# New written orders for TensorE's instruction stream in an attention and expert layer, and the expert weights computed four groups earlier

## What is computed

```python
xn = layernorm(x)                          # x: 2 x 2048 x 256
q, k, v = split(xn @ Wqkv)                 # 16 heads of 16, rotary embedding on q and k
attn = softmax(causal(q @ k.T * scale)) @ v
p = softmax(xn @ gate_w.T + gate_b)        # 10 gates: 8 experts, 2 null ones
w, chosen = top_k(p, 2)                    # null choices weigh nothing, the rest is normalised
ffn = sum over the two choices: w * (xn @ expert_w[chosen] + expert_b[chosen])
out = x + attn @ Wout + bout + ffn
```

## Time and profile before

| | us |
|---|---|
| median of three runs | 1015.39 |
| the profiled execution | 1015.35 |
| span of its instructions | 1013.6 |
| TensorE busy | 909.3 |
| VectorE busy | 846.4 |
| ScalarE busy | 727.5 |
| GpSimd busy | 462.7 |
| `attend`: group 0, first score to that of group 1 | 91.5 |
| group 3 | 106.4 |
| group 6 | 96.2 |
| group 7 | 89.3 |

### The profile page before, as it was taken

The page is one execution under the profiler, slowest core; times in us unless marked ns, Lnnn a source line. Parts: engine busy times, 40 slices in busy tenths (PEclk is TensorE's granted clock), DMA queues, the critical chain, the costliest instruction groups (busy, mean ns, idle before and its releaser), DMA issues. The chain is left out here.

```text
span 1013.6 us, 22104 instructions
## 1 busy us (share of the span) xinstructions
PE 909.3 (90%) x7874; PEld 389.5 (38%) x7874; DVE 846.4 (83%) x1096; ACT 727.5 (72%) x1542; POOL 462.7 (46%) x588
## 2 busy tenths in 40 slices
PE   3888445999999999999999999999999799999988
PEld 1544311333433244344443544353434233323257
DVE  6999789899889988886888788877888599994856
ACT  3556200888778888888888788878887688799922
POOL 4677659555200343344834564255222344355610
PEclk9999765899999999999999999999999899999989
DMA  9776810300200323244413542265323321022113
GB/s 324 267 256 238 285 51 6 111 2 26 68 14 2 106 85 126 78 135 145 126 54 114 151 143 76 70 167 134 82 75 118 97 60 54 23 64 64 43 42 125
DMA packets 82084, 106.65 MB, mean 105 GB/s; under 512 B 10000, under 2 KB 59064, under 8 KB 80952
## 3 DMA queue, kind: packets, MB, share of 16 engines
q1 hardware_dynamic: 74488, 85.83, 26.3%
q0 software_dynamic: 6528, 17.83, 6.7%
q10 hardware_dynamic: 960, 1.57, 0.5%
HBM read 67.37 MB, written 37.50 MB: 103 GB/s over the span
## 5 line engine op out<-in xcount | busy, mean ns | idle before, releaser
L1272 DVE TENSOR_REDUCE blk<-psP 128x2 f32<-128x1024 f32 (+2 forms) x576 | 640.9, 1161 | 102.1 <-PE psP L1415 52.0
L1218 ACT ACTIVATE probs<-psS 128x512 f32<-128x512 f32 (+3 forms) x1280 | 589.0, 540 | 163.8 <-PE psS L1455 157.9
L1455 PE MATMUL psS<-Qs,Ks 50*128 50x512 f16 (+3 forms) x1280 | 331.6, 354 | 13.4 <-ACT probs L1218 8.9
L1415 PE MATMUL psP<-Ks,Qs 48*128 48x512 f16 (+3 forms) x1280 | 295.8, 363 | 27.9 <-DVE blk L1272 17.3
L1511 PE MATMUL psO<-probs,Vs 128*32 128x512 f32 (+3 forms) x2560 | 302.7, 548 | 11.1 <-POOL probs L1119 10.1
L1119 POOL TENSOR_SCALAR_AFFINE_SELECT probs<-probs 128x512 f32<-128x512 f32 x128 | 88.1, 689 | 333.7 <-ACT probs L1218 251.3
L1455 PEld LDWEIGHTS psS<-Qs,Ks 50*128 50x128 f16 x1280 | 96.0, 93 | 252.8 <-ACT probs L1218 157.7
L1415 PEld LDWEIGHTS psP<-Ks,Qs 48*128 48x128 f16 x1280 | 80.1, 95 | 124.1 <-DVE blk L1272 90.0
L1418 PE MATMUL psP<-later,eye 64*128 64x128 bf16 x1024 | 98.3, 223 | 0.0
L1511 PEld LDWEIGHTS psO<-probs,Vs 128*32 128x32 f32 x2560 | 52.3, 109 | 93.2 <-issue 69.3
L1418 PEld LDWEIGHTS psP<-later,eye 64*128 64x128 bf16 x1024 | 75.4, 98 | 19.9 <-issue 1.7
(11 more groups left out here) (170 smaller groups left out, 724.7 us busy)
## 6 DMA issues: line engine op xcount, KB each, us to landing
xn<-we_scratch SPq DMA_DIRECT2D x72, 256.0 KB
expert_scratch<-xn SPq DMA_DIRECT2D x36, 256.0 KB, 2.6
v_scratch<-vst SPq DMA_DIRECT2D x8, 1024.0 KB, 4.0
qk_scratch<-part SPq DMA_DIRECT2D x32, 256.0 KB, 4.0
Vs<-v_scratch SPq DMA_DIRECT2D x16, 512.0 KB, 3.9
Qs<-qk_scratch SPq DMA_DIRECT2D x168, 32.0 KB
Ks<-qk_scratch SPq DMA_DIRECT2D x168, 32.0 KB
acc<-x SPq DMA_DIRECT2D x8, 512.0 KB, 9.1
```

Of the source, the lines that this page charges most:

```text
L1218: nc.scalar.activation(probs[u % NPR][:, h, q0:CH], psS[:, k % SB, q0:CH], ACT.Exp, scale=exp_scale).then_inc(s_read[k % SB], 1)
L1272: nc.vector.tensor_reduce(out, src, AX.X, ALU.max).then_inc(item_ok[slot], 1)
L1415: ins = pe.matmul(psP[:, slot, at:at + w], Qs[r][rows, qt // CT, p, t * P:(t + 1) * P], Ks[r][rows, kc, p, 0:w], start=True, stop=True)
L1455: pe.matmul(psS[:, k % SB, q0:CH], Ks[r][rows, kt // CT, p, kt % CT * P:(kt % CT + 1) * P], Qs[r][rows, c, p, q0:CH], start=True, stop=Tru ...
```

## The change

The four strings are written anew (the `route` one follows from `plain`), and `weights()` moves from the last group to the fourth, g = 3, still behind that group's last `q` or `m`; `add_first()` stays in the last group.

```diff
         PE_ORDER = {
             "plain": (
-                    "ss10s01ssmps10ss01ss01ss01ss10spss01s01sps0s11ss0spss10s01pss01sps0s1s0s1ssp01ss01sps10sp1s0s1s0"
...
-                    "sposs10p01sss10ps10spss10s1s0sspss01s10spmps10ss01sss01p10pssoso"),
+                    "ss10s01sspms10ss1s0s10s1ss01s0sp10sss01p01ssp01sss10ps10ssp01sss10pss0s10s1sp0ss1ps0s110sspsss100"
...
+                    "1s0sposss01p10sss01p1ss0sps0s1ss10sspms0101ssspss10ss1s0pppssoos"),
             "experts": (
-                    "ss1010ssmxps01s1ss0ss10s0s1spss01s1p0ssspss011sps0ssps10s10xy1s0s01xp1s0ssp0s1ss0ys10sps1x0ss1p0"
...
-                    "sspss01spp1ss010yx01s10sp01sspssos10spss01psss10s01ssmyxossps10ss1s0ps1s0s1s0ppyos"),
+                    "1s0s10ssmxps0s1s01ss1s01s0sspss01s1p0sssps10ss1ps0ssps10s10xy01sspss0101sxssp0ss101yss10ps01syx0"
...
+                    "sps01sspps01s10sy01ssoxss10p1s0ss1pss010sppsss10s0s1xmyos01spsss01s1ssps0s1s0ppyos"),
             "last": (
-                    "10s10ssmspss010s1ss10ss01sps01ss01ps10ssps0s11ss0sps10s1sps0s10spss01sss1s0sps01ss0ps1s01ss01ssp"
-                    "ss01ss10ssspss100s1spmssppsssps0s10ss1ss01sspsss1pss01sss0s1s0spssspssps0sss1ss01spssspsssp0s11s"
-                    "0sssspssspssos0s1sp0s1spssspmssspsssssssspsspsspsossspssspssspssssssspsssssspsspppoo"),
+                    "ss101s0ssmps10ss10ss10ss01ss1s0p01sss10p10sssp01ss01sps01ssp01ss01spss10ss10ssp0s11s0sps10sspss0"
+                    "1s10pss0sss1ss1s0smps01ss10sps0s1s01sspsssps01sspss1s01pss0spsss1pss0sps1s0ss0s1sss0s1s01spsssps"
+                    "ssssssmpsspssssspssspsspsssspsosossssssspsspssspssspsspssspsspsssssssspsssssspsspppoo"),
         }
...
                         normalise(j, r, WALK.index(item[2]), item[2], slot)
+                    if g == 3 and n == rest:
+                        weights()
                     if kind == "last" and n == rest:
-                        weights()
                         add_first()
```

More of the change, by code:

```diff
@@ L924, in attend @@
             "plain": (
-                    "ss10s01ssmps10ss01ss01ss01ss10spss01s01sps0s11ss0spss10s01pss01sps0s1s0s1ssp01ss01sps10sp1s0s1s0"
-                    "sp10ssspss10s10sspms10ss10ss01ss01ps01ssp1s0ss10psss01p10sss01p0ss1s01spss1s010sspmsss1001pss10s"
-                    "s01sss01sp01sss10ps10sspsosss01ss01sp01sss10ps10ss0p1sss10psss01p01sss01psss01sss10ssps0s1s01sps"
-                    "sposs10p01sss10ps10spss10s1s0sspss01s10spmps10ss01sss01p10pssoso"),
+                    "ss10s01sspms10ss1s0s10s1ss01s0sp10sss01p01ssp01sss10ps10ssp01sss10pss0s10s1sp0ss1ps0s110sspss100"
@@ L929, in attend @@
+                    "ss1ps01ss0sss1ssmps0s10ss1s10ss0s1p0s1sp10sss01ps10s1ss0p01sss01p0s1spsss01s10sspms01ss0s1s01s1s"
+                    "0ps01ss10ssp10sss01ps10ssps01pss01s10ssp0ss1s1p0ss01spss01s10sps10ssoss10s1s0ssps01ss0ss1p0ss1sp"
+                    "1s0sposss01p10sss01p1ss0sps0s1ss10sspms0101ssspss10ss1s0pppssoos"),
             "route": "",
             "experts": (
-                    "ss1010ssmxps01s1ss0ss10s0s1spss01s1p0ssspss011sps0ssps10s10xy1s0s01xp1s0ssp0s1ss0ys10sps1x0ss1p0"
@@ L932, in attend @@
-                    "s1s01y0ss1ps01ss0sss1sspms01s0s1ss10ss01ssp01ssps1s01sp0s1s0sps1ss0pss0110xys01sps0s1s01ssxmps1s"
-                    "010sspss0s1s0s1ssps01ss10y10ss01ps10ssps0s1ssp10sss01pssos10sp01sspssx01s10sps10syss01pss01sss01"
-                    "sspss01spp1ss010yx01s10sp01sspssos10spss01psss10s01ssmyxossps10ss1s0ps1s0s1s0ppyos"),
+                    "1s0s10ssmxps0s1s01ss1s01s0sspss01s1p0sssps10ss1ps0ssps10s10xy01sspss0101sxssp0ss101yss10ps01syx0"
+                    "10ss1ps01sspss1s0ss10sssmps10s1ss0s10ss1ps0s10sps0s1sps0s10sps10s1sp01sssps10ss01xys0s1s0s1xmps0"
@@ L935, in attend @@
+                    "s1s01spss10ss10ssps0s1s01y01ss01ps10ssps10sssp01ss10spsso1ss0ps10spssx1010ssps10sy01sspss10s0s1s"
+                    "sps01sspps01s10sy01ssoxss10p1s0ss1pss010sppsss10s0s1xmyos01spsss01s1ssps0s1s0ppyos"),
             "last": (
-                    "10s10ssmspss010s1ss10ss01sps01ss01ps10ssps0s11ss0sps10s1sps0s10spss01sss1s0sps01ss0ps1s01ss01ssp"
-                    "ss01ss10ssspss100s1spmssppsssps0s10ss1ss01sspsss1pss01sss0s1s0spssspssps0sss1ss01spssspsssp0s11s"
-                    "0sssspssspssos0s1sp0s1spssspmssspsssssssspsspsspsossspssspssspssssssspsssssspsspppoo"),
+                    "ss101s0ssmps10ss10ss10ss01ss1s0p01sss10p10sssp01ss01sps01ssp01ss01spss10ss10ssp0s11s0sps10sspss0"
@@ L939, in attend @@
+                    "1s10pss0sss1ss1s0smps01ss10sps0s1s01sspsssps01sspss1s01pss0spsss1pss0sps1s0ss0s1sss0s1s01spsssps"
+                    "ssssssmpsspssssspssspsspssspsosossssssspsspssspssspsspssspsspsssssssspsssssspsspppoo"),
         }
```

## The result

The changed kernel takes 1018.57 us (median; 1016.34 to 1021.20). The kernel before, measured beside it, takes 1015.96 us. The ratio is 1.0026, with a 95% interval of 1.0015 to 1.0037: it is slower by about a quarter of a per cent, and no change lies outside the interval. The forecast was 1014.3 us, about no change. Its range of 1009.0 to 1018.8 holds the result, its direction is wrong.

A forecast was written before the change was run, and what follows sets the result against it. VectorE was taken to bound the plain groups, TensorE groups 2 to 5, and waits to hold group 7. Fourth group +5.6, last group -6.3, orders -0.4 gave -1.1 us against 1015.35, so 1014.3 us; range 1009.0 to 1018.8.

The forecast's parts named there:

- The weights in group 3: Group 3 into 4: weights delay normalising the last `o`, so TensorE's item 1 waits; 4.1 us plus 1.5 for clock lost.
- The gain of the last group: Group 7: earlier sums remove TensorE's 4.25 us wait for a mask and pv at the low clock; 6.3 us gained.
- the starved mask's end: End of group 7: a GpSimd mask took 7.19 us beside VectorE's sums; its 4.25 us wait of TensorE would go.
- My forecast takes 0 here: Group 7, units 28 to 31: masks meeting the moved sums cost nothing; one that loses would cost up to 2.2 us.
- the held-back pv: Group 7: the new string holds the pv of unit 28 until 32.25 units, leaving 11.6 us before its mask is wanted.
- The starved mask as a rival: Group 7: a unit 28 mask or gather loses to the sums; 2.2 us wait plus 1.2 clock, 1017.7 us; chance 0.25.
- The orders: New strings, all groups: only the experts' entries count, 4 x 0.10 = 0.4 us gained; waits allowed 0.5 us a group.
- Counting entries and neighbours: TensorE's strings: counts of entries into all-row work and same-side neighbours per group; experts' entries go from 50 to 49.
- The wait in group 6: Group 6: TensorE's 4.84 us idling ahead of a pv stays, since 15 scores and seven items still precede it.
- The Trainium skill's rule of the lock: VectorE and GpSimd lock shared ports per instruction; a mask waits for one sum, 0.4 us, and none is starved.

The follow-up runs named there:

- the upper heap of the old orders' runs: Kernel before with weights and sums both spread, old orders kept: ratio 1.0010; its timed runs lay in two heaps, the upper at 1015 to 1017 us.

## Why the prediction was wrong

The forecast added +5.6 (group 4), -6.3 (last group) and -0.4 (orders). In the two profiles these terms came out as +6.2, +0.7 and -8.0, with another +3.0 in the first and the output stage, which the change doesn't touch: +1.9 by these roundings. That the time lies inside the range is luck: the last group missed by 7.0 us one way and the orders by 7.6 the other, about 2 of these by chance (groups 1 and 6).

- **The weights in group 3: right.** Forecast 4.1 us of shift and 1.5 for the clock, 5.6 in all. The wait is 4.12 us, the group loses 6.2 with the new orders and 5.4 with the old. Slot, waiting item and engine are as written.
- **The gain of the last group: the step that failed.** The prediction took 6.3 us for the starved mask's end and wrote "My forecast takes 0 here" for what the new place would cost. The 6.3 is 5.8 by the run without sums. The zero was wrong twice. A mask was starved again. And the new order is longer in itself: 1.5 us by unit 28 and 1.0 from there to unit 32, by the timelines with and without sums, apart from the clock. The starved mask adds 2.5 us up to unit 32, and the low clock behind it 1.5. With 84.6 these make the 91.1. I had priced the held-back pv as what gives the mask time, and not as what ScalarE waits for, though the four buffers were in my own description of the kernel. Some 0.8 of the 1.5 us come before unit 23, ahead of both held-back pv; I don't know what they are.
- **The starved mask as a rival.** It came, with chance 0.25 given, and gave 1017.7 for the measured 1018.57, close by luck: it held neither the length of the new order nor the gain in the other groups. Its wait was 1.59 us for the 2.2 allowed. TensorE's wait was the wrong measure: ScalarE's was 3.68.
- **The orders: too small, and wrong in the last group.** Forecast 0.4 us. By the means of all profiles, old orders against new (without the low clock in group 1 and the groups that the weights lengthen), groups 0 to 5 gain 0.6, -0.2, 1.4, 1.7, 1.9 and 0.5 us, 5.9 in all. Group 6 gains nothing: 96.2 us with either order, since the 95.1 of the changed kernel's profile came with a short wait. Counting entries and neighbours told nothing of this. It isn't the waits either, which I had bounded at 0.5 us a group: in group 3 TensorE's busy time falls from 103.57 to 102.56 us, 1.0 of the 1.6. What in the strings does it stays open.
- **The wait in group 6: right.** It stayed (3.68 us in the changed kernel). Its price, the wait and 1.5 us, came out as the wait and 2.1, by a kernel that moves the gathers and the weights' steps too.
- **The Trainium skill's rule of the lock** (SBUF — State Buffer, "SBUF: two separate sides") holds in what it says of one instruction: where the sums are spaced, no mask is over 0.92 us. The forecast's 0 took it to hold against a queue of sums as well, and there the measurement decides: in five of six profiles with the sums in a block, one instruction of GpSimd lost against 14 to 22 sums in a row.
- **Left open.** The projection stage (+1.6 us) and the output stage (+1.4) differ between profiles of kernels that are equal there: the output takes 39.2 or 40.7 us, in step with whether the clock is low in its first 3.4 us. What decides that was not found. Nor was what makes the upper heap of the old orders' runs.

## What to carry over

A block of work on an engine with time to spare isn't free: ask what stands behind it in that engine's queue and who needs that within the block's length. Here a block of 6 us cost 5.4 and 6.2, and one of 13 cost 2.5 to 7.6 in six profiles, against the same order without it. Laid one by one into gaps that the profile shows, the same instructions cost 0.7 to 2.3 us in the better places, and 4.2 to 5.1 in others, so the places have to be tried. An order that holds a step back to make room for a late input also holds back whoever waits for that step's buffer, so it is to be tried once with the late input taken away.

## What was new about the hardware

- Of GpSimd's masks that met 32 back-to-back sums with two inputs in SBUF, 13 got in within 0.4 us, but in five of six profiles one instruction was starved to the end of the block: a mask in four (7.19, 6.45 and 6.94 us, and 6.45 in the kernel with the weights spread), the issue of a gather in the fifth (9.70 us). In the sixth, the new orders alone, none was. In six profiles with a wait between the sums the longest mask was 0.92 us; where these sums stand together they took 0.59 us each in place of 0.42 on average (18.82 and 13.30 us for the 32).
- TensorE's granted clock fell to 1.2 GHz not only with waits of 1.6 to 5.6 us, but also near unit 23, where it ran scores and half items with waits of at most 0.21 us between them in the rows and its last pv lay 2.8 to 3.4 us back. The same instructions left the clock up in two of seven profiles. Without a wait of TensorE of 5.6 us a group was 7.7 us shorter.
